# Rows of the first attention group made in place by TensorE products instead of by transfers, and the Hadamard transform moved from the prologue to the last batch

## Time and profile before

| | us |
|---|---|
| median of 3 runs | 586.02 |
| lowest, highest | 585.2, 586.32 |
| the profiled execution's own time | 586.26 |
| its span in the profile | 584.4 |

### The profile page before, as it was taken

How to read it: one execution, slowest core, us unless ns; L and a number is a source line. 1 busy time by engine, 2 the same in 40 slices (tenths; PEclk the granted TensorE clock), 3 DMA queues, 4 the chain that set the end, 5 groups by cost and what they waited for, 6 DMA issues and landing times.

```text
span 584.4 us, 8867 instructions
## 1 busy us (share of the span) xinstructions
PE 565.8 (97%) x3288; PEld 390.1 (67%) x3288; DVE 376.8 (64%) x718; ACT 298.5 (51%) x546; POOL 176.6 (30%) x193
## 2 busy tenths in 40 slices
PE   9899999999999988999999999999999999999997
PEld 4534334344334433368888888898777888888886
DVE  5498898898888899644363444558887436344433
ACT  3238878876886787752334242244445233424221
POOL 3956446354455242820101010014333010101000
PEclk9999999999999999999999999999999999999999
DMA  7654740240033030010000000000000010010101
GB/s 231 135 112 163 199 122 18 76 127 20 2 111 109 3 146 3 3 72 2 1 0 1 1 0 1 2 2 0 1 0 2 1 36 1 1 36 2 38 0 37
DMA packets 17891, 26.54 MB, mean 45 GB/s; under 512 B 2552, under 2 KB 10744, under 8 KB 17464
## 3 DMA queue, kind: packets, MB, share of 16 engines
q1 hardware_dynamic: 15992, 24.13, 13.6%
q10 hardware_dynamic: 1856, 1.84, 1.4%
HBM read 10.88 MB, written 5.24 MB: 28 GB/s over the span
## 4 chain that ended last, share of the span: by engine, by line
PE 85%; DVE 5%; ACT 4%; issue 2%; DMA 1%; POOL 1%; SPq 1%; DVEq 0%; ACTq 0%
PE PS L281 82%; PE PS L292 2%; DVE mxr L861 2%; ACT PR L735 1%; DMA ring<-ql 1%; DVE PR L1020 1%; ACT xf L644 1%; ACT qf L658 1%; DVE XNs L842 1%; ACT PR L788 1%; POOL xTl L1051 1%; ACT xTh L644 1%; PE PS L472 1%; DVE AOl L853 1%; SPq L214 1%
## 5 line engine op out<-in xcount | busy, mean ns | idle before, releaser
L281 PE MATMUL PS<-xTh,ring 128*128 128x512 f32 x608 | 188.5, 392 | 0.0
L861 DVE TENSOR_REDUCE mxr<-PS 128x1 f32<-128x512 f32 x256 | 163.0, 682 | 29.0 <-PE PS L281 28.7
L735 ACT ACTIVATE PR<-PS 128x512 f32<-128x512 f32 x256 | 137.8, 603 | 39.7 <-PE PS L281 39.7
L281 PEld LDWEIGHTS PS<-xTh,ring 128*128 128x128 f32 x608 | 113.2, 188 | 22.9 <-issue 0.8
L281 PE MATMUL PS<-xTl,ring 128*128 128x512 f32 x304 | 110.3, 391 | 0.4 <-POOL xTl L1051 0.4
L281 PE MATMUL PS<-ring 50*128 50x512 f32 (+1 forms) x512 | 98.2, 450 | 5.4 <-DVE mxr L861 4.9
L975 DVE TENSOR_TENSOR PR<-PR,PS 128x512 f32<-128x512 f32 x64 | 43.8, 684 | 91.6 <-PE PS L281 73.7
L281 PEld LDWEIGHTS PS<-ring 50*128 50x128 f32 (+1 forms) x512 | 41.2, 184 | 84.2 <-ACT PR L735 57.2
L644 ACT ACTIVATE AOh<-PR 128x512 fp32r<-128x512 f32 x72 | 45.5, 632 | 101.1 <-DVE PR L975 89.2
L1051 POOL TENSOR_TENSOR xTl<-xf,xTh 128x512 fp32r<-128x512 f32 x30 | 43.2, 1456 | 140.9 <-ACT xTh L644 140.9
L853 DVE TENSOR_TENSOR AOl<-PR,AOh 128x512 fp32r<-128x512 f32 x72 | 51.1, 710 | 50.3 <-ACT AOh L644 50.3
(11 more groups left out here) (98 smaller groups left out, 621.5 us busy)
## 6 DMA issues: line engine op xcount, KB each, us to landing
ring<-qh SPq DMA_DIRECT2D x52, 128.0 KB, 3.1
ring<-ql SPq DMA_DIRECT2D x26, 128.0 KB, 3.1
ring<-weight_scratch SPq DMA_DIRECT2D x3, 1024.0 KB, 4.9
weight_scratch<-in_w SPq DMA_DIRECT2D x2, 1024.0 KB, 6.8
out<-X SPq DMA_DIRECT2D x8, 256.0 KB, 2.2
X<-in_x SPq DMA_DIRECT2D x3, 512.0 KB, 5.2
PR<-in_w SPq DMA_DIRECT2D x1, 1024.0 KB, 7.6
ring<-AOh SPq DMA_DIRECT2D x8, 128.0 KB, 4.0
```

The lines of the kernel that those rows point to most:

```text
L281: return nc.tensor.matmul(dst, lhsT, rhs, start=start, stop=stop, skip_group_check=True)
L735: nc.scalar.activation(PR[:, j % 8, :], PS[:, kq_bank(j), :], ACT.Exp, scale=HD ** -0.5)\
L861: nc.vector.tensor_reduce(mxr[:, S % 2, blk, TT * p + t:TT * p + t + 1], PS[:, QK0 + i % 3, :], AX.X, ALU.max, negate=True).then_inc(max_d ...
```

## The change

Nothing changes in what is computed. The change does six things.

1. **Stack products.** For pairs 0 and 1 of batch 0, queries and keys, weights are spread over 48 of 64 columns (each channel three times, rest zero) in the tiles W2h and W2l, which are free at that time. One product of six passes (`project_rows`) then gives all rows in place. ACT writes `mask * (product + bias)` rounded (`stack_hi`), and DVE writes `product + bias - that` into `ring` (`stack_rows`): high rows where the mask is 0, low rows where it is 1. Masks come from the identity, and biases by eight small transfers (`sbias`, `rbias`). Four such stacks, two before the first maxima and two beside units U = 0 and 1.
2. **Rest rows.** Queries and keys of pairs 2 and 3 come from one product of six passes (`REST_BANK`) and 12 transfers of half the size (`rest_rows`), which are waited for at U = 8.
3. The tiles n = 2 and 3 and the values move from before the maxima to beside them (`beside_maxima`), in place of fills and Hadamard products; `keep_busy(7)` at the start becomes `keep_busy(4)`.
4. Batch 1's normalising moves from POOL to ACT (two steps a tile); the low parts of the projection weights move from DVE to POOL.
5. Wo's eight loads move from ACT's queue to SP's, ahead of the two layouts; its split moves to K = 3 (ACT) and K = 5 (POOL).
6. The Hadamard transform moves to the last attention batch: W2 comes in two halves (into qf from s = 20 of batch 2, and into vst at s = 3 of the last batch), butterflies on POOL at s = 3, 5, 7, 9, 11 (`FLY_AT`), products on PE at s = 14, 16, 26, 28 (`HAD_AT`), evacuated by ACT and POOL (the first two) and by DVE (the last two).

The core of the diff:

```diff
-HAD_AT = (4, 5, 6, 8)
+HAD_AT = (14, 16, 26, 28)
+FLY_AT = (3, 5, 7, 9, 11)
@@ sync
+            sp.dma_start(ident[:, :], ident_d).then_inc(ident_in, DMA)
             sp.dma_start(qf[:, 0, :]...).then_inc(wq_in, DMA)
-            sp.dma_start(ident[:, :], ident_d).then_inc(ident_in, DMA)
-            sp.dma_start(PR[:, 0:4, :]..., w2...).then_inc(w2_in, DMA)
-            sp.dma_start(had[:, :], had_d).then_inc(w2_in, DMA)
             sp.dma_start(X[:, TT:2 * TT, :], xv[1, :, :, :]).then_inc(x_in[1], DMA)
+            sp.wait_ge(sbias_set, 1)
+            ... 4 x sp.dma_start(sbias[...]), 4 x sp.dma_start(rbias[...]) .then_inc(sbias_in, DMA)
...
-            ring_load(0, 0)
-            for n in range(2):
-                sp.wait_ge(ring_in[n], QDMAS)
+            sp.wait_ge(qk_hi, 2)
+            for args in rest_rows(QI, 0):
+                sp.dma_start(*args).then_inc(ring_in[0], DMA)
+            sp.wait_ge(qk_lo, 2)
+            for qk in range(2):
+                for args in rest_rows(qk, 1):
+                    sp.dma_start(*args).then_inc(ring_in[qk], DMA)
             ring_load(0, 2)
-            ring_load(0, 3)
+            ring_load(0, 3, (0,))
             max_rows(0)
+            ring_load(0, 3, (1,))
+            ... 8 x sp.dma_start(OT[...], wo[...]).then_inc(wo_in, DMA)
...
+                    if b == BATCH - 2 and s == QK_AT[3][-1] + 4:
+                        sp.wait_ge(qk_lo, 4 * BATCH)
+                        ... had and the first half of w2 into fly_raw(0) = qf, w2_in[0]
+                    if b == BATCH - 1 and s == 3:
+                        sp.wait_ge(vp_ready, LAST_GROUP)
+                        ... the second half of w2 into fly_raw(1) = vst, w2_in[1]
@@ tensor
-            keep_busy(7, MB, SEQ)
+            keep_busy(4, MB, SEQ)
...
-            keep_busy(1, MB, SEQ)
-            for n in range(4): ... project_qk(0, n, range(6), PS[:, QK_BANK[n], :])
-            ... project_v, keep_busy(2), wait ring_in[0], keep_busy(3), wait qk_hi 4, qk_lo 4
+            keep_busy(1, MB, FILL)
+            pe.wait_ge(pad_done, 1)
+            pe.wait_ge(swlo_done, 1)
+            project_stack(0)
+            pe.wait_ge(swlo_done, 2)
+            project_stack(1)
+            pe.wait_ge(rwlo_done, 1)
+            project_rows(lambda lo, kt: rest_weights(lo)[:, kt, :], REST_BANK, False).then_inc(qk_ready, 2)
+            def beside_maxima(U):
+                if U < 2:
+                    project_stack(2 + U)
+                elif U < 6:
+                    n = 1 + U // 2
+                    ... project_qk(0, n, range(3 * (U % 2), 3 * (U % 2) + 3), PS[:, QK_BANK[n], :])
+                elif U < 10:
+                    ... (at U == 9 the transpose of the first maxima)
+                    project_v(0, (U - 6) // 2, U % 2, PS[:, V_BANK[(U - 6) // 2], :])
+                elif U == 11:
+                    ... ln_transpose(0, MB)
+                if not more and s in HAD_AT:
+                    j = HAD_AT.index(s)
+                    if j == 0:
+                        pe.wait_ge(fly_done, 5)
+                        pe.wait_ge(mt_ready, turned // 8)
+                    elif j == 2:
+                        pe.wait_ge(x_done, 2 * b)
+                    else:
+                        pe.wait_ge(w2h_done if j == 1 else w2l_done, j)
+                    mm(MB, had[:, :], fly_half(j // 2)[:, j % 2 * SEQ:(j % 2 + 1) * SEQ], True, True)
@@ vector
+            dve.wait_ge(mask_done, 1)
+            dve.wait_ge(sbias_in, 8 * DMA)
+            nc.vector.tensor_tensor(sbm[:, :, :], sbias[:, :, :], smask..., ALU.mult).then_inc(sbm_done, 1)
             for dt in range(KD):
                 dve.wait_ge(x_hi, dt + 1)
                 lo(xTl[:, 0, dt, :], PS[:, dt, :], xTh[:, 0, dt, :]).then_inc(x_lo, 1)
...
+                nc.vector.scalar_tensor_tensor(ring[:, 0, w, p, :], PS[:, STACK_BANK[i], :], sbias[:, p, w:w + 1],
+                                               stack_tmp(i).bitcast(F32), ALU.add, ALU.subtract).then_inc(stk_done, 1)
@@ gpsimd
-            ... three butterfly stages in the prologue
+                if b == BATCH - 1 and s in FLY_AT:
+                    i = FLY_AT.index(s)
+                    ... i = 0, 1: stages on the first half; 2, 3: on the second half; 4: across the halves
```

More of the change, by code:

```diff
@@ L313, in project_qk, with project_rows, project_stack @@
                     last.then_inc(qk_ready, 1)
+            def project_rows(weights, bank, first):
+                ops = [(1, 1, 0), (0, 1, 0), (1, 1, 1), (0, 1, 1), (0, 0, 0), (0, 0, 1)]
+                for i, (lo, r, kt) in enumerate(ops):
+                    if first and lo:
+                        pe.wait_ge(x_hi, kt + 1)
+                    if first and not r:
+                        pe.wait_ge(x_lo, kt + 1)
+                    last = mm(PS[:, bank, :], weights(lo, kt), xt(0, kt)[r], i == 0, i == 5)
+                return last
+            def project_stack(i):
+                p, w = i // 2, i % 2
+                project_rows(lambda lo, kt: stack_weights(lo, w)[:, kt, p * P:(p + 1) * P], STACK_BANK[i], i == 0)\
+                    .then_inc(stk_ready, 1)
             def project_v(b, half, part, bank=MB):
@@ L716, in _ @@
[L716 to L724 removed]
+            weights_hi(0)
@@ new lines, in _ @@
+            act.wait_ge(sbm_done, 1)
+            stack_hi(0)
+            weights_hi(1)
+            stack_hi(1)
+            weights_hi(2)
+            act.wait_ge(qk_ready, 2)
+            nc.scalar.activation(qh[:, 0, :], PS[:, REST_BANK, :], ACT.Identity, bias=rbias[:, :]).then_inc(qk_hi, 2)
+            act.wait_ge(qk_hi, 2)
+            for i in (1, 0):
+                act.dma_start(*rest_rows(KI, 0)[i]).then_inc(ring_in[1], DMA)
+            stack_hi(2)
+            for i in (3, 2):
+                act.dma_start(*rest_rows(KI, 0)[i]).then_inc(ring_in[1], DMA)
@@ new lines, in _ @@
+            stack_hi(3)
+            act.wait_ge(nmean_done, 1)
+            act.wait_ge(rstd_done, 2)
+            act.wait_ge(lnT_ready, 2)
+            for t in range(TT):
+                nc.scalar.activation(XNs[:, t, :], X[:, TT + t, :], ACT.Identity, bias=nmean[:, t:t + 1])\
+                    .then_inc(centred, 1)
+            act.wait_ge(bias_in, 2 * DMA)
+            first_split(2)
+            for t in range(TT):
+                c = slice(TT + t, TT + t + 1)
+                act.wait_ge(centred, t + 1)
+                last = nc.scalar.activation(XNs[:, t, :], XNs[:, t, :], ACT.Copy, scale=rstd[:, c])
@@ L1096, in output_lo, with fly @@
                 lo(AOl[:, 2 + (n - 1) % 2, :], AOf[:, :], AOh[:, 2 + (n - 1) % 2, :]).then_inc(aol_done, 1)
+            def fly(first, second, total, difference):
+                nc.gpsimd.tensor_tensor(total, first, second, ALU.add)
+                nc.gpsimd.tensor_tensor(difference, first, second, ALU.subtract).then_inc(fly_done, 1)
             def add_bo(b):
@@ L1105, in _ @@
             nc.gpsimd.memset(Vp[:, :, :, HD:HD + 1], 1.0).then_inc(pool_init, 1)
+            for part in range(2):
+                v = (W2h, W2l)[part][:, 0:4, :].bitcast(F32).rearrange("p f n -> p (f n)")\
+                    .rearrange("p (g n) -> p g n", n=HALF)[:, :, KROWS:]
+                last = nc.gpsimd.memset(v, 0.0)
+            last.then_inc(pad_done, 1)
             nc.gpsimd.memset(Vp[:, :, :, HD + 1:], 0.0).then_inc(vone_done, 1)
@@ L1136, in _ @@
             x_lo_part(1, 0, 0)
+            for g in range(1, GROUPS):
+                place_values(0, g)
             for K in range(STEPS * BATCH):
```

349 lines of the change are left out of this document (221 added, 128 removed).

## The result

| | before | changed |
|---|---|---|
| median of 11 runs, us | 586.02 | 589.17 |
| lowest, highest | 584.81, 586.95 | 585.39, 591.43 |
| granted clock, mean of a run | | 0.981 to 0.991 |
| profiled execution, us (span) | 586.26 (584.4) | 591.38 (589.6) |

The ratio is 1.0046, with a 95% interval of 1.0031 to 1.0062. The changed kernel's spread of 6 us is new, and it goes with the clock column: 591.4 at 0.981 and 0.982, 589.2 to 589.5 at 0.984 and 0.985, about 588 at 0.987 and 0.988, 585.4 and 585.8 at 0.991. The profiled execution is one of the slowest. Its rows explain the 591.38; only this run was profiled, so of the others the mean clock says how much low clock they had, not where.

A forecast was written before the change was run, and what follows sets the result against it. PE was taken to bound the kernel, with DVE's maxima setting the pace before the main loop. Terms -11.0 + 1.0 + 2.8 + 1.7 = -5.5 took 586.26 to 580.7 us (580.5 on the median's scale); range 576 to 584.5.

The forecast's parts named there:

- Opening fills: Kernel start: with four fills PE is free near 7.45 us, and the first pass on x starts at 9.7 instead of 12.40.
- Biases: Prologue: DVE waits for eight small transfers, taken to land at 10.5 us (between 9.5 and 17); first scores at 15.0.
- Maxima: Stage before the main loop: DVE stays the bound, 18.8 us from first scores, main loop at 33.8, 11.0 us earlier.
- First batch: First attention batch: waiting for Wo's loads (0 to 2.5 us) and the later layouts (0 to 1) costs 1.0 us together.
- Butterflies: Last batch: POOL's five steps take 15.0 us and end near 230.0, so PE stands 2.8 us at s = 14.
- Products: Last batch: four fp32 Hadamard products on PE, 0.89 us each, partly hidden, cost 1.7 us together, ends 0 and 3.6.
- Slower, by the granted clock: Rival, 9%: PE idles from 9.7 to 15 us, the clock falls to 1.2 GHz and stays; about 594 us.
- Butterflies in time: Rival, 17%: PE reaches s = 14 later, or the wait for Wo is nothing; about 577 us.
- prologue late: Rival, 22%: biases land near their upper bound or a row transfer is late at U = 8; 583 to 585 us.

The follow-up runs named there:

- the two fill experiments: Changed kernel with 12 small fp32 products inside the s = 14 wait, 586.67 us; changed kernel with fill products at U = 10 and 12, 584.61 us.
- the kernel with the fills ahead of the loop: Changed kernel with a fill product of 384 columns beside each of U = 10 and U = 12: 584.61 us, ratio 0.9985.
- the kernel with the three edits: Changed kernel with x's low parts ahead of DVE's bias wait, fills at U = 10 and 12, and Hadamard products at s = 16 and 17: 580.03 us.
- the first experiment: Changed kernel with the first two Hadamard products at s = 16 and 17 in place of 14 and 16: 582.54 us, ratio 0.9951.
- the profile with the low parts moved: Changed kernel with one edit, DVE making x's two low parts before it waits for the biases: 583.69 us, ratio 0.9983.
- the three edits without fills: Changed kernel with x's low parts ahead of the bias wait and Hadamard products at s = 16 and 17, no fills at U = 10 and 12: 580.87 us.
- the wait filled: Changed kernel with 12 small fp32 products on the identity inside the wait for the butterflies at s = 14: 586.67 us, ratio 1.0019.
- The four profiles of the wait at s = 14: Changed kernel, and it with the wait filled, with fills at U = 10 and 12, or with low parts ahead of biases: s = 13 to 21 took 15.05 to 19.62 us.

## Why the prediction was wrong, point by point

The sum was -5.5 us, the profiled execution came out at +5.1 and the median at +3.1, and the range was missed. By the milestones:

- **The step that failed** is the pricing of PE's idle time by its own length, with the clock set apart as a rival of 9%. The prediction let that rival start from the prologue before 15 us alone, and dismissed it with 1.65 us of idleness in a transfer wait without a drop. The changed kernel has 1.76 us in one piece, and the prediction itself forecast 2.8 us in the last batch, well beyond what it had called harmless, without asking the clock about it. What the runs showed in its place: of the 9.7 us between the sum at full clock and the measured +5.1, 4.0 were low clock in the first batch, 2.7 low clock in the last one, and 3.0 a main loop that started at 38.17 in place of 35.0 to 35.4, behind the long wait for the biases and its low clock.
- **The sum at full clock.** This is an estimate from the rows: main loop 9.4 to 9.8 earlier (35.41 and 35.02, in the profiles of the two fill experiments, which had no fall before 34.6), first batch 0, wait at s = 14 1.2, products 3.8. That gives about -4.6 where the forecast had -5.5, some 581.6 us, inside the range. The two runs of the kernel with the fills ahead of the loop that had clock 1.000 took 582.1 and 583.0.
- **Where luck helped.** The kernel with the three edits came out at 580.03 (-6.1 us of span), half a us from the 580.5 of the forecast, but it is no proof of the sum: it has no wait at s = 14 (forecast at 2.8), nothing in the first batch (1.0), a gain of 9.7 in place of 11.0 at the loop, and products at 3.8 in place of 1.7. The errors cancel.
- **Opening fills.** 2.7 us forecast for the first product on x, at 9.7; it came at 10.16, 2.2 earlier than before. Seven fills against four in one kernel make 2.4 on this product and 2.2 in the whole.
- **Biases.** Forecast to land at 10.5, ends 9.5 and 17; DVE went on at 11.8, and the last four took 3.2 to 3.8 us from issue. The size was inside, the reading not: the wait stood on DVE ahead of something PE needed, and cost PE the 1.76 us of idleness that the clock answered. First scores at 18.45 in place of 15.0; 15.57 with the low parts moved ahead, so 2.9 of the 3.4 us are this wait's and its clock's. The spread weights' copies, which were to end by 9.5, ended at 10.6 on DVE and did not delay the low parts.
- **Maxima.** 18.8 us forecast; 19.7 in the changed kernel, 19.5 with the three edits. Right in kind, 0.7 to 0.9 small. DVE stood 0.80 us for ACT's rows of the third stack (0.43 with the three edits); the prediction put nothing for it. In the changed kernel's profile ACT was held by its two row transfers (issued until 20.9, stack at 20.92), with the three edits by PE's product. And the stage did not end on DVE alone: PE's last wait before the loop is 0.88 us for the load of the first maxima, which SP issued at 35.43 behind four row transfers. The prediction had it landing 0.8 us before the loop.
- **First batch.** 1.0 us for Wo's loads and the layouts: nothing. 8.14 us from loop to s = 5 with the moved transfers in place (43.18 - 35.04), the same as before. What the changed kernel lost there, 4.0 us, was clock alone.
- **Butterflies.** Forecast: PE stands 2.8 us at s = 14. It stood 2.59, put down to POOL, with POOL without a gap (the prediction's own terms give 2.9, 230.0 less 227.1). The observation was right to 0.2 us and its price wrong twice: at full clock the wait is worth 1.2 us, since half is caught up; with the low clock 2.7 more.
- **Products.** 1.7 us forecast with ends 0 and 3.6; measured 3.8 by stretches, 2.6 for the first two. The slack of 0.43 us every second step that the prediction subtracted is there, but with the products at s = 16 and 17 PE waits 0.51 us for ACT's evacuation between the two and 0.37 us for POOL's split behind them (the rows of the first experiment), which it didn't count.
- **Rivals.** "Slower, by the granted clock" was the one that came, at two further places than it named, and at +5.1 instead of +8. The clock did not stay low as it had assumed: in the profiles each fall lasted 3.4 to 10.2 us. "Butterflies in time" did not come; "prologue late" did in its smaller part, by the 1.3 us of the biases (11.8 in place of 10.5).

The Trainium skill ("TensorE: Matmul & The Clock Gate", Part 1) says that an idle TensorE falls back to 1.2 GHz; the trace agrees, with a fall behind 1.76 us of idleness and one within 2.59. That 1.65 us in one piece before had no such effect is in the trace too:

```profile
24.48 2.84 PE L281 MATMUL PS<-AOf 128*128 128x512 f32 x6 [1.65 <-DMA ring<-ql]
```

What sets a harmless 1.65 us apart from 1.76 us with a fall, no run here shows.

## What to carry to other kernels

When a change takes work or fills away from TensorE, list each new idle piece of it and ask for each what the next 3 to 10 us of TensorE work would cost at half the clock; here three waits of 0.9 to 2.6 us turned a gain of some 4.6 us (the estimate above) into a loss of 3. A fill that costs nothing on the path (two of 0.64 us), a consumer placed two steps later, or a wait moved behind the work that others need took the price away here. And if a kernel's runs spread where those of the kernel before didn't, compare each run's time with its own granted clock before looking for anything else. And when an experiment lands on the forecast, check the terms before the total.

## What the runs showed of the hardware that was not expected

- Small idle pieces can be enough: 0.26 and 0.88 us within 3 us, PE busy 2.65 of the 3.80 us from 34.80 to 38.60, stood ahead of a fall that lasted to 49 us, and with two fills of 0.64 us no run of the kernels with the three edits had it. They need not be: the profile with the low parts moved has 0.26 and 0.22 us and a fall at 35.2, and the one of the three edits without fills has 0.25 and 0.61 us and none. The length of a piece alone predicts nothing here.

```profile
34.80:38.60 3.80, 2.65 (x14) 1.00 0.40 134
```

- The same kernel gets its falls in some runs and not in others; whole runs of one kernel lay up to 8.3 us apart (579.87 and 588.15 with the products at s = 16 and 17). The kernel before is not quite immune: of the 57 runs of it made beside the experiments one had a mean clock of 0.996, and it was the longest, 587.53 us. A part of the changed kernels' spread is the prologue's timing: with the same instructions up to there, PE stood 1.76 and 1.79 us for x's low part in the profiles of the changed kernel and of the first experiment, and the clock fell; it stood 0.39 us with the wait filled and 0.53 us with the fills ahead of the loop, and the clock stayed until 34.6 us or longer. Nor does the wait of 2.6 us at s = 14 always bring a fall: two of the twelve runs with the fills ahead of the loop, which keep this wait, had clock 1.000.
- A us at the lower level costs about half a us here: the runs of the changed kernel at a mean clock of 0.991 took 585.6 us (two runs), those at 0.981 and 0.982 took 591.4 (three). The difference of 0.0093 in the mean is 0.019 of the time at half speed, 11 us, and the times differ by 5.8. The four profiles of the wait at s = 14 give 0.4 to 0.45.
- A tiny product on DVE can last as long as a big one on POOL. sbm (128x4) takes 0.16 us in the two profiles where it runs before POOL begins the low part of a projection weight (128x512, 1.3 us), and 0.65 to 1.21 us in the nine others, where POOL is in it; there both end within 0.03 us of each other. In the kernel with the three edits ACT's idle 1.44 us ahead of the first stack end with it, so the wait was in part only moved. No experiment puts sbm ahead of POOL's work.

```profile
11.48 1.21 DVE L1046 TENSOR_TENSOR sbm<-sbias,smask 128x4 f32<-128x4 f32 x1
```

- The opening's low clock is missing from the row of granted clocks: the profile of the kernel before gives 1.00 for 1.44 to 5.87 us, where the fill passes took 0.89 us each against 0.45 later. The record of the clock starts after the opening, and the mean of 0.999 leaves it out.
